# Residual add of the FFN on VectorE, straight behind the product with the gate row, instead of on GpSimd

## What is computed

```
h = layernorm(x) * (1 + cb) + sb
gate = quantised(h) @ quantised(w_gate)^T        # 512 -> 1408
up   = quantised(h) @ quantised(w_up)^T          # 512 -> 1408
y    = quantised(silu(gate) * up) @ quantised(w_down)^T   # 1408 -> 512
out  = x + gb * y
```

## Time and profile before

| | us |
|---|---|
| median of 3 runs | 2052.4 |
| lowest and highest run | 2047.46, 2056.08 |
| the profiled execution | 2050.25 |
| its span | 2048.4 |
| TensorE busy | 1949.7 (95%) |
| VectorE busy | 1612.1 (79%) |
| GpSimd busy | 1058.9 (52%) |
| ScalarE busy | 619.2 (30%) |

### The profile page before, as it was taken

The page is one execution under the profiler, slowest core; times in us unless marked ns, Lnnn a source line. Parts: engine busy times, 40 slices in busy tenths (PEclk is TensorE's granted clock), DMA queues, the critical chain, the costliest instruction groups (busy, mean ns, idle before and its releaser), DMA issues.

```text
span 2048.4 us, 27228 instructions
## 1 busy us (share of the span) xinstructions
PE 1949.7 (95%) x9401; PEld 926.3 (45%) x9401; DVE 1612.1 (79%) x2080; ACT 619.2 (30%) x878; POOL 1058.9 (52%) x1083
## 2 busy tenths in 40 slices
PE   4889999999997999999999999999999999999996
PEld 2334444444443444444444444444444444444442
DVE  4768686868676888888888888888888888888884
ACT  2234343434322223223222232232232232222321
POOL 2255455555543556555555565565565555655641
PEclk7999999999999999999999999999999999999998
DMA  6845646554732433434334334334334333343342
GB/s 253 286 114 162 177 145 164 154 159 140 171 107 78 89 70 77 96 69 86 87 69 92 81 69 102 71 72 102 69 79 93 69 85 88 69 93 79 69 94 49
DMA packets 417862, 219.19 MB, mean 107 GB/s; under 512 B 356214, under 2 KB 356226, under 8 KB 417804
## 3 DMA queue, kind: packets, MB, share of 16 engines
q1 hardware_dynamic: 417804, 218.44, 42.7%
HBM read 96.48 MB, written 33.57 MB: 63 GB/s over the span
## 4 chain that ended last, share of the span: by engine, by line
PE 47%; issue 15%; DVE 14%; DMA 8%; POOL 7%; SPq 4%; ACT 2%; DVEq 0%; ACTq 0%; POOLq 0%
PE bank L883 22%; PE bank L830 14%; PE bank L904 11%; DMA arena<-arena 6%; DVE arena L1205 2%; SPq L355 2%; POOL arena L560 2%; SPq L412 2%; POOL arena L578 2%; DVE arena L1165 1%; DVE arena L1172 1%; DVE arena L1153 1%; DVE arena L1134 1%; PE bank L855 1%; ACT arena L698 1%
## 5 line engine op out<-in xcount | busy, mean ns | idle before, releaser
L883 PE MATMUL bank<-wgu_hi,arena 128*128 128x512 f16 (+1 forms) x3072 | 876.4, 362 | 22.6 <-DMA arena<-arena 22.3
L883 PE MATMUL bank<-wgu_lo,arena 128*128 128x512 f16 (+1 forms) x1536 | 556.0, 362 | 0.0
L830 PE MATMUL bank<-arena,wq_hi 128*128 128x512 f16 x1536 | 461.9, 383 | 16.1 <-DMA arena<-arena 9.3
L883 PEld LDWEIGHTS bank<-wgu_hi,arena 128*128 128x128 f16 x3072 | 300.9, 98 | 342.8 <-DVE arena L1172 21.7
L904 PE MATMUL bank<-wd_hi,arena 128*128 128x512 f16 x1408 | 430.9, 380 | 16.1 <-DMA arena<-arena 16.1
L830 PE MATMUL bank<-arena,wq_lo 128*128 128x512 f16 x768 | 293.6, 382 | 0.0
L904 PE MATMUL bank<-wd_lo,arena 128*128 128x512 f16 x704 | 267.6, 380 | 0.0
L586 POOL TENSOR_TENSOR arena<-arena,h_minus 128x1 f32<-128x1 f32 x64 | 97.8, 1529 | 320.5 <-DVE arena L1198 320.5
L830 PEld LDWEIGHTS bank<-arena,wq_hi 128*128 128x128 f16 x1536 | 150.8, 99 | 196.2 <-issue 16.1
L725 ACT ACTIVATE arena<-arena 128x1408 bf16<-128x1408 f32 x64 | 88.1, 1377 | 500.0 <-DVE arena L1205 500.0
L904 PEld LDWEIGHTS bank<-wd_hi,arena 128*128 128x128 f16 x1408 | 138.2, 98 | 185.0 <-DMA arena<-arena 18.3
(11 more groups left out here) (129 smaller groups left out, 2596.1 us busy)
## 6 DMA issues: line engine op xcount, KB each, us to landing
arena<-in_L_attn_x_dram SPq DMA_DIRECT2D x32, 1024.0 KB, 6.0
arena<-x_scratch SPq DMA_DIRECT2D x128, 256.0 KB, 2.7
x_scratch<-arena SPq DMA_DIRECT2D x16, 1024.0 KB, 4.3
out_dram<-arena SPq DMA_DIRECT2D x64, 256.0 KB, 2.2
arena<-in_L_wmod_dram SPq DMA_DIRECT2D x6, 1024.0 KB, 8.9
arena<-in_L_attn_W_qkva_dram SPq DMA_DIRECT2D x1, 3072.0 KB, 15.3
wgu_hi<-in_L_ffn_w_gate_dram SPq DMA_DIRECT2D x1, 2816.0 KB, 13.3
wgu_lo<-in_L_ffn_w_up_dram SPq DMA_DIRECT2D x1, 2816.0 KB, 10.6
```

The source lines that it names most:

```text
L830: last = pe.matmul(dst[m % 2][:, :].rearrange("p (j t) -> p j t", j=NJ), w[:, k, at], uT[p][:, half, :, k, :], start=(n == 0), stop=(n == ...
L883: last = pe.matmul(dst[n][:, 0:w], xT[p][:, half, k, :], wt[:, k, cut], start=(m == 0), stop=(m == 3 * KD - 1))
```

## The change

`ffn_add_x` leaves GpSimd's program. VectorE has a function of the same name that does the same addition on the same buffers and raises the same count, and calls it straight behind each `gate_out`. It waits for the residual and for its own product, which has just been issued. Nothing else is edited; line numbers behind it shift by nine.

```
--- before.py
+++ after.py
@@ -591,12 +591,6 @@
-                def ffn_add_x(i, p):
-
-                    pool.wait_ge(gated_ready, i + 1)
-                    wait(pool, x_res_loaded[p], 8 * (i - p) + 16)
-                    pool.tensor_tensor(gated[p], gated[p], x_res[p], ALU.add).then_inc(x2_ready, 1)
@@ -615,11 +609,8 @@
                         ffn_adaln(i + 3, 1 - p, b3)
-                    if not (isinstance(i, int) and i < 1):
-                        ffn_add_x(i - 1, 1 - p)
 
                 tiles(pool, tile)
-                ffn_add_x(NTA - 1, 1)
@@ -1231,6 +1222,12 @@
                     dve.scalar_tensor_tensor(gated[p], d_bank[p][:, :], fst[:, p, DSC], gb[:, b, :],
                                              ALU.mult, ALU.mult).then_inc(gated_ready, 1)
+
+                def ffn_add_x(i, p):
+
+                    wait(dve, x_res_loaded[p], 8 * (i - p) + 16)
+                    dve.wait_ge(gated_ready, i + 1)
+                    dve.tensor_tensor(gated[p], gated[p], x_res[p], ALU.add).then_inc(x2_ready, 1)
@@ -1330,10 +1327,12 @@
                     if not (b == 0 and first):
                         gate_out(i - 1, 1 - p, b - first)
+                        ffn_add_x(i - 1, 1 - p)
 
                 tiles(dve, tile)
                 h_lo(NTA - 1, 1)
                 gate_out(NTA - 1, 1, B - 1)
+                ffn_add_x(NTA - 1, 1)
```

## The result

| | before | after |
|---|---|---|
| median | 2054.66 us (5 runs, the first three among them) | 2066.38 us (5 runs) |
| lowest, highest | 2047.46, 2056.08 | 2062.79, 2068.41 |
| ratio to before | | 1.0063, interval 1.0042 to 1.0084 |
| span of the profiled execution | 2048.4 | 2066.3 |

The change makes the kernel 11.7 us slower by the medians; 12.5 us were forecast. The ratio is worked out from all runs of both kernels and not from the two medians, whose quotient is 1.0057. The loss is clear of noise, but whether it is over the half per cent that the prediction calls "slower" is not settled, since the interval starts at 1.0042.

The account below looks back on a forecast made before the run. The FFN was taken as bound by a cycle through VectorE and TensorE, 43.39 us for two tiles. 13.5 us longer in the loop minus 1.0 at the end, 12.5 us on 2052.4, gave 2065 us, range 2050 to 2071.

Parts of the forecast that it names:

- The two cycles: FFN loop, two tiles: 43.39 us through TensorE, 42.89 on VectorE alone; after the change 43.84 and 43.79.
- the push of 0.45: GpSimd's L567, behind the addition, makes VectorE's low half of x (L1165) end 0.45 us later per two tiles.
- The addition is hidden, the turn is not: VectorE's addition fits the 1.41 us idle time, but its turn ahead of L567 delays L1165's end by 0.45 us.
- Order of the turns: A waiting VectorE instruction with two SBUF inputs gets in between two of GpSimd, so the addition precedes L567.
- 30 pairs, 13.5 us: FFN steps 1 to 60 of 64: 30 pairs of tiles at 0.45 us each, 13.5 us longer.
- The removal: Taking L598 off GpSimd: 0 in the loop; at the end 0.58 and 0.42 us, together 1.0 us shorter.
- The idle time of TensorE for the transposition in nearly every tile: Sign in the profile after: TensorE waits for the transposition in nearly every tile rather than every second.
- L1225 unchanged or shorter in the trace: Sign in the profile after: VectorE's L1225 lasts as long or shorter, since it starts later.
- A (the cover holds): Rival: the addition doesn't wait for L578, or doesn't push L1165; loop stays 43.39 us, 2051.4 us; chance 0.17.
- B's orders: Rival: GpSimd keeps L578 and L567 together; +17 us (chance 0.09), or +49 us if L569 goes first (0.04).
- C's reason: Rival: GpSimd loses its longest loop instruction, L598, which lies on the chain, so faster, 2041 us; chance 0.05.
- VectorE is simply full: Rival set in the follow-ups: VectorE, at 84% before, has no room for 0.7 us more a tile; no chance given.

Follow-up runs that it names:

- psum_input: Changed kernel, its addition reading the down product in PSUM instead of the gated product in SBUF: 2050.42 us, ratio to before 0.9987.
- half_add: Changed kernel with its addition on only the first 256 of the 512 columns: 2054.98 us, ratio to before 1.0020.
- add_alone: Kernel before, GpSimd keeping its add, with VectorE making the same addition as well into spare space: 2064.09 us, ratio to before 1.0055.
- removal_alone: Changed kernel with no residual addition on any engine: 2050.92 us, ratio to before 0.9991.
- add_in_gap: Changed kernel with VectorE's addition moved to the next step, behind the layernorm statistics, where GpSimd is idle: 2049.63 us, ratio to before 0.9992.

## Why the prediction was right

Taking its steps in order:

- **The two cycles.** Confirmed: 43.39 us with the push of 0.45 gave 43.85, and the run that relieved only VectorE's cycle showed TensorE's at 43.83. The prediction had 43.84 for the cycle through TensorE and 43.79 for VectorE's own and said the first remains the longer. That small step failed: the chain of the changed kernel runs through VectorE's own, which is as long. It did not matter for the sum, since the two differ by hundredths, but nothing in the prediction said that they would come out level.
- **The addition is hidden, the turn is not.** Confirmed in each term: 0.55 and 1.13 us from the release, L567 ends 1.68 behind L578 instead of 1.23, the low half of x at 1.46 to 1.53 us. That the second SBUF input is the cause is shown by psum_input, and that the length of the turn sets the size by half_add.
- **Order of the turns.** The waiting VectorE instruction did get in between L578 and L567, as L1225 had between L569 and L598. And L569 got in between L1156 and L1216, although L1216 was issued 0.08 us before L1156's end. The first happens some 60 times in each profile where the two lines meet, and so does the second: in these traces a waiting instruction of either engine comes ahead of the next one of the other.
- **30 pairs, 13.5 us.** From the first L1165 beside GpSimd to the product with the gate row ahead of the last low half of x it is 1986.64 - 660.51 = 1326.1 us before and 2004.77 - 666.26 = 1338.5 us after: 12.4 us more. add_alone has 13.5 us more there. The regular pairs agree; about 1 us of the difference between the two runs lies in the one pair where the batch changes (43.97 us in the changed kernel, 44.95 in add_alone, 44.51 before), for a reason that these runs don't show. The forecast by the median was 2065 us, 2066.38 was measured.
- **The removal.** Worth nothing in the loop, as said. Its two parts at the end are in the trace: the last low half of the hidden values takes 1.62 us instead of 2.04 (0.42), and the last addition ends 1.55 us behind the start of its product instead of 2.09 (0.54, where 0.58 was forecast). But they did not arrive as 1.0 us: from that same product to the end of the span it is 61.8 us before and 61.5 after. The last down product took 10.07 us instead of 9.41. In both kernels it starts at a granted clock of 0.50 (1.2 GHz), behind 13 us without work, and it was at full clock 4.2 us after its start before the change and 5.6 us after it. (In add_alone, where the last add is still GpSimd's, this end is 61.5 us as well.) So a term of this size can't be told from the spread of single profiles, and that 12.4 - 0.3 = 12.1 us lies so near the 12.5 forecast is in part luck.
- **Two signs missed.** "The idle time of TensorE for the transposition in nearly every tile" came only in part: 37 stops for a transposition instead of 29; the other 17 of its 54 stops are for VectorE's hidden values (L1163), since VectorE's own cycle had become as long. And "L1225 unchanged or shorter in the trace" was wrong: L1216 takes 2.69 us instead of 2.43. It does end 0.45 us later, as worked out, but it is issued at once behind L1156 instead of after an idle time of 0.18 us, so more of its wait for the turn is inside its own record.
- **Rivals.** A (the cover holds) would have been right had the addition read PSUM, or stood in the other gap. B's orders did not occur. C's reason is refuted by removal_alone. "VectorE is simply full" is refuted by psum_input and add_in_gap, where VectorE does 44 and 39 us more in all than before and the time is not longer.

## What to carry to other kernels

Before moving an instruction into an idle time, ask not only whether it fits but whom it takes a turn from, and who waits for that one: here 0.7 us fitted into 1.4 us and still cost 0.45 us on the path of each two tiles. Where GpSimd and VectorE are both busy, look for records that last longer than the same instruction does alone, and lay their ends beside the other engine's ends; such a record on the chain may be a gain to be had, here by one wait on the engine that has time (0.5% for one line on the kernel before). And find the cycle that sets the period, with everything on it: relieving a part that only one of two level cycles uses gives nothing.

## What the runs showed of the hardware

The taking of turns was more exact than expected. From the other engine's end to its own end a waiting VectorE instruction took 0.28 us for 256, 0.55 for 512 and 1.48 for 1408 elements, a waiting GpSimd one 1.13 us for 512 and 0.05 us for one column, within 0.02 us wherever one waited for the other in the eleven profiles. The elements alone don't decide: the same 512 with one input in PSUM ran beside GpSimd at full speed (0.69 us, psum_input). One pair in the trace of before overlaps without cost: GpSimd's L558, on one column, lasts from 1417.40 to 1417.95, and L1215, with two SBUF inputs, is issued at 1417.61 and still takes its usual 1.62 us; so a record's end need not be the very end of the turn. A wait for the turn shows in no list of waits; it is in the instruction's own time, also for a GpSimd instruction on one column, which lasts 1.48 us in the earlier trace rows.
